# Where VectorE's and ScalarE's side work stands within the rounds of an attention stage

## The reference

```python
x = x + _L0_attn_ref(_layernorm(x), Wqkv, bqkv, Wo, bo)     # changed here
x = x + _L0_ffn_ref(_layernorm(x), gate_up_packed, ...)     # FP4 weights, unpacked during the attention
x = x + _L1_attn_ref(_layernorm(x), W_in, W_out, decay, bias)   # a recurrence
x = x + _L1_ffn_ref(_layernorm(x), gate_w, w_gate, ...)     # 64 experts, the best 6 of each token

scores = einsum('bsnh,btnh->bnst', k, q) / sqrt(HEAD_SIZE)
scores = triu(scores) + -10000.0 * tril(ones, k=-1)
attn = softmax(scores, axis=2)
out = einsum('bnkq,bknh->bqnh', attn, v)

nib = w[:, :, None] >> shifts & 15            # FP4 weight: a code of 4 bits
vals = _FP4_LUT[nib] * scale                  # times a scale for each group of 128
```

## Time and profile before

| | |
|---|---|
| time, median of 3 runs | 1811.92 us (1809.47 to 1814.84) |
| span of the profiled execution, first to last instruction | 1799.4 us |
| median less that span | 12.5 us |
| TensorE busy, whole span | 1662.0 us (92%) |
| VectorE, ScalarE, GpSimd busy, whole span | 1103.2, 703.2, 587.6 us |
| stretch from 200 to 540 us (nearly all of the attention): TensorE, VectorE, ScalarE, GpSimd busy | 320.29, 217.94, 187.53, 140.06 of 340.00 us |
| granted TensorE clock in this stretch, share of full speed | 0.98 |

### The profile page before, as it was taken

One profiled execution on the slowest core, in us unless ns is written; L12 is line 12 of the kernel. 1 busy time (PEld: TensorE's weight loads), 2 busy tenths in 40 slices (PEclk: granted clock), 3 DMA queues, 4 the chain that ended last, 5 costly groups with the idle time before them and its releaser, 6 DMA issues. The chain is left out here.

```text
span 1799.4 us, 22628 instructions
## 1 busy us (share of the span) xinstructions
PE 1662.0 (92%) x7201; PEld 1177.9 (65%) x7201; DVE 1103.2 (61%) x2382; ACT 703.2 (39%) x1330; POOL 587.6 (33%) x859
## 2 busy tenths in 40 slices
PE   6997899999989899999967999999699999999995
PEld 5886454555547677777755767677477777777774
DVE  5444766666736778787878567797544444444442
ACT  3211455555552455555442142212044334433442
POOL 3001333433551334444445051121133333333322
PEclk9998799999999999999988999999899999999998
DMA  7344456556623500000010031102799999999994
GB/s 253 115 141 134 139 159 156 160 161 162 164 70 108 188 1 1 1 1 1 1 59 33 0 119 51 47 21 72 254 325 354 338 357 351 345 345 350 353 354 91
DMA packets 120679, 284.83 MB, mean 158 GB/s; under 512 B 23472, under 2 KB 35248, under 8 KB 120304
## 3 DMA queue, kind: packets, MB, share of 16 engines
q1 hardware_dynamic: 106224, 247.71, 40.0%
q0 software_dynamic: 14336, 35.66, 9.0%
HBM read 224.03 MB, written 54.69 MB: 155 GB/s over the span
## 5 line engine op out<-in xcount | busy, mean ns | idle before, releaser
L897 ACT ACTIVATE probs<-bank 128x512 f32<-128x512 f32 (+3 forms) x384 | 167.6, 503 | 185.4 <-PE bank L840 183.9
L2000 POOL DMA_INDIRECT out_x<-e_y,row_out x64 | 104.0, 1626 | 316.4 <-DMA out_x<-e_y,row_out 174.1
L2035 PE MATMUL bank<-w_gate,xgt 128*128 128x352 f32 x512 | 163.7, 463 | 0.0
L2035 PE MATMUL bank<-w_up,xgt 128*128 128x352 f32 x512 | 161.9, 459 | 0.0
L2101 DVE TENSOR_TENSOR e_hidden<-e_silu,bank 128x352 f32<-128x352 f32 x64 | 33.4, 522 | 201.4 <-issue 181.6
L815 PE MATMUL bank<-k_stack,q_stack 96*128 96x512 f32 (+2 forms) x360 | 136.2, 391 | 22.2 <-DMA k_stack<-qk_parts 11.8
L1200 PE MATMUL bank<-ln_xt_hi,gu_codes 128*128 128x512 f32 x352 | 145.6, 414 | 10.8 <-DVE gate_sum L1273 5.3
L854 PE MATMUL bank<-probs,v_ones 128*64 128x512 f32 (+3 forms) x768 | 142.1, 506 | 6.7 <-POOL probs L764 6.7
L940 DVE CUSTOM_DVE_ANT_0 masked_scores<-bank,wide_mask 128x128 bf16<-128x128 f32 (+1 forms) x240 | 109.3, 482 | 63.5 <-PE bank L815 62.8
L840 PE MATMUL bank<-q_stack,k_stack 98*128 98x512 f32 (+3 forms) x384 | 141.0, 382 | 2.1 <-ACT probs L897 1.8
L764 POOL TENSOR_SCALAR_AFFINE_SELECT probs<-probs 128x128 f32<-128x128 f32 x256 | 77.9, 321 | 196.5 <-ACT probs L897 192.4
(11 more groups left out here) (261 smaller groups left out, 3842.2 us busy)
## 6 DMA issues: line engine op xcount, KB each, us to landing
w_gate<-in_w_gate SPq DMA_DIRECT2D x64, 704.0 KB, 6.7
w_up<-in_w_up SPq DMA_DIRECT2D x64, 704.0 KB, 7.8
w_down<-in_w_down SPq DMA_DIRECT2D x64, 512.0 KB, 8.7
q_stack<-qk_parts SPq DMA_DIRECT2D x96, 128.0 KB, 3.8
k_stack<-qk_parts SPq DMA_DIRECT2D x96, 128.0 KB, 4.0
w_down<-in_w_down SPq DMA_DIRECT2D x64, 192.0 KB, 10.0
qk_parts<-qk_stage_hi SPq DMA_DIRECT2D x32, 256.0 KB, 2.0
qk_parts<-qk_stage_lo SPq DMA_DIRECT2D x32, 256.0 KB, 2.3
```

The lines of the kernel that those rows point to most:

```text
L897: act.activation(probs[u % PROBS][:, 0:cols], m.bank[EXPB[u % 3]][:, 0:cols], ACT.Exp, scale=scale).then_inc(exp_ready, 1)
L2000: pool.indirect_dma_start(out=a["out"][:, :], out_offset=bass.IndirectOffsetOnAxis(ap=row_out[e % YS][:, :], axis=0), in_=y[e % YS][:, :], ...
L2035: last = pe.matmul(m.bank[bank[e % 2]][:, 0:F], xt[e % 2][:, k, :], w[e % R][:, k, :], start=(k == 0), stop=(k == KT - 1))
```

## The change

Eight pieces of work keep what they do and get other places in the order of their engine. On VectorE the two bit steps, the low part and the inversion go from places within rounds (after the maxima of units 2, 6, 13 and 22) to the ends of the four rounds (after those of units 5, 11, 17 and 23). On ScalarE the high part goes from the fifth place of round 0 to the start of round 1, the second half of the output copy from the third place of round 1 to its start, behind the high part, the codes from the fifth place of round 2 to its start, and the first half of the output copy from the third place of round 3 to its start.

```diff
             for p in range(PAIRS):
                 for r in range(ROUNDS):
                     for n in range(EXP_ROUND):
-                        if n == 2 and r == 1 and p >= 1:
+                        if n == 0 and r == 1 and p >= 1:
+                            dq.scalar_hi(act, p - 1)
                             copy_out(p - 1, 1)
-                        if n == 2 and r == 3:
+                        if n == 0 and r == 2:
+                            dq.scalar_codes(act, p)
+                        if n == 0 and r == 3:
                             copy_out(p, 0)
-                        if n == 4 and r == 0 and p >= 1:
-                            dq.scalar_hi(act, p - 1)
-                        if n == 4 and r == 2:
-                            dq.scalar_codes(act, p)
                         exponential(p, EXP_ROUND * r + n)
...
                 for n in range(U):
                     maxima(ahead[len(ahead) * n // U:len(ahead) * (n + 1) // U])
-                    if n == 2:
+                    if n == EXP_ROUND - 1:
                         dq.vector_gu_bits(dve, p)
-                    if n == 6 and p >= 1:
+                    if n == 2 * EXP_ROUND - 1 and p >= 1:
                         dq.vector_lo(dve, p - 1)
-                    if n == 13:
+                    if n == 3 * EXP_ROUND - 1:
                         dq.vector_down_bits(dve, p)
-                    if n == 22 and p >= 1:
+                    if n == 4 * EXP_ROUND - 1 and p >= 1:
                         invert(p - 1)
```

## The result

The changed kernel takes 1818.01 us in the median of 17 runs (1812.16 to 1828.34), the kernel before 1811.96 us in 17 runs taken beside them (1801.62 to 1822.76). The ratio is 1.0042 with an interval of 1.0023 to 1.0062: 6.05 us slower, where 4.2 us were forecast. It is also more than the 0.3% from which a difference counts here, an outcome that had a chance of 0.31; the interval reaches to both sides of that bound.

The account below looks back on a forecast made before the run. Bound: TensorE's path and the inversion-to-stack-load loop, equally long. Twelve loops x 0.37 = +4.4, -0.5 first reader, -0.5 slack, +0.8 clock: +4.2, 1811.9 to 1816.1 us; 8-in-10 range 1808.5 to 1821.5.

Parts of the forecast that it names:

- The bound: TensorE's own path (20.77 us a pair) and the loop inversion, store, read-back, stack loads end together at a row-maximum product.
- Low part: VectorE, round 1: moving it to the round's end frees banks sooner and shortens TensorE's own path by 0.48 us per pair.
- Inversion: VectorE, end of round 3: one step later starts it 0.37 us later (0.16 to 0.61), lengthening each of twelve loops.
- Gate/up bits: VectorE, round 0: moving the two instructions to the round's end costs 0, as they still precede the next round's first read.
- The wait at M12: TensorE's row-maximum product, first reader of the loaded stacks, waits 0.6 to 0.9 us in nearly all of pairs 2 to 13.
- Rival B: Stack loads on SyncE gain from later stores and arrive early enough; round 1's gain stays: 1805.7 us, chance 0.12.
- Rival D: Code store stands nearer ahead, so each store of the inverse takes 2.06 us: +11, 1823 us; chance 0.18.
- Clock: Longer stalls before the stacks' first reader may cause one more fall of TensorE's clock: 0 to 1.8 us, taken as 0.8.
- ScalarE at no cost: High part, codes and two output copies move to round beginnings, where ScalarE idles for TensorE: cost 0.
- Around the program: 12.5 us between the profiled span, 1799.4 us, and the median, 1811.9, taken as lying around the program.
- the first M12: The first reader of the stacks, whose load came long before, comes 0.48 us earlier: -0.5 us.
- the slack: Four pairs whose stack load was in time give up their 0.1 us or a little more once: -0.5 us.

Follow-up runs that it names:

- the loop open: SyncE's store and read-back of the inverse moved behind the next stack loads: ratio 0.9941 in the kernel before, 0.9933 in the changed kernel, both against the kernel before.

## Why the prediction held, point by point

- *The range.* The measured time lies in it, and so would no change at all: the range reached from 1808.5 to 1821.5 us around a time before of 1811.9. The number alone bears nothing out; the runs above do.
- *The bound.* Right. Two paths of nearly equal length end at M12; with the loop open, M12 waits in no pair, and with it closed and TensorE's path shortened, in all.
- *Low part.* Right: 0.48 us a pair were forecast; 0.50 show up in the pair without a wait, 0.51 with the loop open, and the low part alone brings it.
- *Inversion.* Right, and slightly short: +0.37 us were forecast, M12 to inversion went from 8.23 to 8.63 us, +0.40. Alone, it made the kernel 5.9 us slower, against 12 x 0.40 = 4.8. Its profile shows no fall of the clock behind an M12, so a clock term is not shown for it.
- *Gate/up bits.* Right in ordinary pairs, wrong in pair 14, where they were put at nothing and gave 0.8 to 1.0 us. The reasoning looked at the banks that M3 to M5 free, not at how long the bits themselves take beside GpSimd.
- *The wait at M12.* 0.6 to 0.9 us were forecast in nearly all pairs; it came in all twelve, from 0.39 to 2.10, mean 1.0, and only three of them lie between 0.6 and 0.9.
- *Rival B* (loads early enough) needed landings under 3.6 us for the load that M12 waits for. The prediction used the median of all 72, 4.1 us; the last loads took 4.50 before and 4.18 after, in the mean, and two of the twelve came under 3.6. Beside 4.50, the 4.0 us of pair 1 spoke for B and not against it. The 0.3 us are a little of B, or scatter: in the kernel with the inversion back, whose store of the low part goes out as late, they took 4.60. *Rival D* needed 2 us for the inverse's store: the median stayed 1.4, and over the thirteen pairs the gap from this store to its read-back is 1.62 us in the mean, 1.66 before. Its condition did not come about either: the code store stands 2.8 us ahead in the mean, after and before, and once 0.70, where the landing took 1.8. Single pairs reach 2.5 after and 3.1 before; the two longest are those of pairs 3 and 9 in both profiles. What makes these late is open.
- *Clock.* The mechanism was right, its size too small for the profiled execution. One fall more was reckoned at 0.8 us; the profile has three more, 4.5 us. Each adds about 1.5 us between M12 and the inversion (10.1 to 10.2 instead of 8.63 us). They follow stalls of 1.00, 2.10, 1.40 and 1.21 us, not only those near 2 us. Stalls of 1.04, 1.14 and 1.24 us were followed by none, nor were 1.47 and 1.83 us in the kernel with the inversion alone, and which stall is followed by a fall stays open. How often it happens in the other executions of this kernel is not seen directly. The granted clock over a whole execution is 0.959 to 0.964 in the seventeen of after; the kernel before has 0.964 to 0.972 in the 52 executions beside the experiments, which points the same way but names no stage.
- *ScalarE at no cost.* Right in ordinary pairs: from 200 to 560 us exponent products waited 1.0 us in all for ScalarE, 1.8 before. Wrong at one place. The reasoning looked at who needs the accumulator banks in an ordinary pair and not at the end of the stage, where the joins have no cover: +2.1 us at pair 14, of which pair 15 gives some 0.7 back (its 24 exponent products take 14.31 us instead of 15.02).
- *Around the program.* The 12.5 us were wrong: 1.8 us lie around a span, and the profile of before was at the quick end of the spread. It did no harm, since the sum was added to the median.

Put together: 4.8 for the inversion, -0.5 for the first M12, -0.3 for the slack, -1.0 and 2.1 in pair 14 and -0.7 in pair 15 make 4.4 us, and 6.05 were measured, with an interval of 4.2 to 11.2. The terms that the forecast lacked nearly cancel, 0.4 us net in pairs 14 and 15; that the number came so near without them is luck. The rest, 1.7 us, would be the clock less what loads gain by landing sooner, but the spread of the runs hides terms of that size. In the profiled executions, from the first M12 of pair 1 to that of pair 13, 263.13 - 256.60 = 6.5 us were measured. From M12 to the inversion 9.3 us are added (4.8 by the inversion's step, 4.5 by the clock), from the inversion to the landing 2.5 are taken away (12.75 us in the mean, 12.96 before), and the slack between landing and M12 takes 0.3.

## What to carry to other kernels

Where a product waits for a load, follow the load back through its queue to what releases it: if that goes back to an earlier product of the same engine, there is a loop, and an instruction that looks idle at its own place (here a reciprocal of 0.24 us) can lengthen every pair by being one step later. Making the engine's own path shorter turned into waits here until that loop was cut, and cutting it took five lines of the queue's order. An edit that is free in each ordinary pass must also be followed through the first and the last pass, where the cover is missing: here one lost 2.1 us there and another gave 1.0.

## What the runs showed of the hardware that was not expected

VectorE's joins at pair 14 have at most 16 elements a partition. They take 0.80 us beside GpSimd's scaling (0.85), and 1.12 and 1.19 beside its sums (1.26 us each for the first two), when GpSimd has begun first. Before, the first two came first and took 0.23 and 0.18; the third began 0.12 us behind the scaling and took 0.76, where it takes 0.18 in an ordinary pair. Each of these four held joins ends 0.02 to 0.03 us after the GpSimd instruction beside it: a wait for that instruction, not a share of speed. The gate and up bits show more of it: L530 of pair 14 (3.32 us before, 1.70 after) and of pair 13 (0.98 before, 2.45 in the kernel with the loop cut open alone) ends each time 0.38 to 0.39 us after a GpSimd instruction, in three of the four after the last of an unbroken row of six or more. Why it got in after the first in the fourth is open. The Trainium skill (SBUF — State Buffer, section SBUF: two separate sides) says that GpSimd and a VectorE instruction that reads two inputs from SBUF, or runs in a 2-port mode, share one port pair as an exclusive lock, and that who starts first keeps it for the whole instruction; the durations here agree. Which mode the second join and the bits ran in, no row shows. No run took GpSimd's work away, so the lock is read from these rows and not isolated.

With the loop open, the store of the inverse (8 KB), issued right behind the twelve loads, landed in a median of 3.7 us (3.2 to 4.3, on the kernel before) and 4.5 us (3.8 to 5.5, on the changed one), against 1.4 us where only the code store is ahead. SyncE stood at the read-back until it had landed; no product waited for it.
